# A fused attention and expert kernel: where four kinds of products stand in each place of the turn, and one half of the router's transposes a turn later

## The reference, cut to what matters

```python
h = jnp.concatenate([_L0_tok_ref(x, ...), txt], axis=1)          # 8 x 384 x 256
n = _layernorm(h)
c_kv = n @ W_DKV ; k = c_kv @ W_UK ; v = c_kv @ W_UV ; q = n @ W_UQ
probs = softmax(where(causal, q @ k.T / sqrt(16), -inf))         # 16 heads of 16
h = h + (probs @ v) @ W_O
m = _layernorm(h)
scores = softmax(m @ router_w) ; the two best of 8 experts for each token
h = h + sum over the two of weight * expert(m) + bias            # 384 slots an expert and choice
```

## Time and profile before

| | before |
|---|---|
| median of 3 runs | 693.08 us (690.37 to 693.27) |
| the profiled execution's own time | 693.07 us |
| its span | 691.3 us |
| TensorE busy | 622.6 us, 90% of the span |
| VectorE / ScalarE / GpSimd busy | 407.3 / 374.7 / 386.3 us |
| chain that ended last, TensorE's share | 64% |

### The profile page before, as it was taken

How to read it: one execution, slowest core, us unless ns; L and a number is a source line. 1 busy time by engine, 2 the same in 40 slices (tenths; PEclk the granted TensorE clock), 3 DMA queues, 4 the chain that set the end, 5 groups by cost and what they waited for, 6 DMA issues and landing times.

```text
span 691.3 us, 13802 instructions
## 1 busy us (share of the span) xinstructions
PE 622.6 (90%) x5104; PEld 510.8 (74%) x5104; DVE 407.3 (59%) x1005; ACT 374.7 (54%) x800; POOL 386.3 (56%) x605
## 2 busy tenths in 40 slices
PE   2888999998989999998878699999999999999990
PEld 2554565565656666565657699999999999999990
DVE  4787686797987979669737144444444444444310
ACT  4456776757676575665541355555544455554430
POOL 3403233336463454546474588888888888887222
PEclk9999999999999999999989899999999999999996
DMA  7339274533423232343121532444444444442222
GB/s 263 100 104 259 67 197 151 171 101 114 136 81 94 74 94 82 96 145 129 35 69 67 185 126 32 101 110 108 105 107 108 107 107 107 106 105 46 23 26 27
DMA packets 66476, 73.73 MB, mean 107 GB/s; under 512 B 6312, under 2 KB 61458, under 8 KB 66408
## 3 DMA queue, kind: packets, MB, share of 16 engines
q1 hardware_dynamic: 55584, 59.27, 28.4%
q0 software_dynamic: 9504, 13.00, 11.1%
q10 hardware_dynamic: 1320, 0.57, 0.3%
HBM read 31.62 MB, written 22.35 MB: 78 GB/s over the span
## 4 chain that ended last, share of the span: by engine, by line
PE 64%; DVE 6%; ACT 5%; issue 5%; POOL 3%; DMA 2%; SPq 1%; ACTq 0%; DVEq 0%; POOLq 0%
PE t_bank L1643 19%; PE bank L1658 12%; PE s_bank L1658 6%; PE bank L669 5%; PE t_bank L634 3%; PE s_bank L612 3%; PE t_bank L727 2%; PE t_bank L697 2%; PE s_bank L1629 2%; DVE mx L1100 1%; SPq L400 1%; PE s_bank L613 1%; PE bank L681 1%; ACT part L975 1%; PE bank L759 1%
## 5 line engine op out<-in xcount | busy, mean ns | idle before, releaser
L1602 DVE TENSOR_TENSOR hl<-h,hh 128x384 fp32r<-128x384 f32 x128 | 102.8, 804 | 157.4 <-ACT h L1560 157.4
L537 POOL TENSOR_SCALAR_AFFINE_SELECT pt<-pt 128x256 f32<-128x256 f32 x192 | 80.3, 423 | 162.6 <-ACT pt L916 126.5
L1100 DVE TENSOR_REDUCE mx<-s_bank 128x2 f32<-128x256 f32 (+2 forms) x192 | 121.9, 681 | 39.3 <-PE s_bank L613 39.0
L1557 ACT ACTIVATE hh<-t_bank 128x384 fp32r<-128x384 f32 x128 | 63.0, 492 | 133.7 <-PE t_bank L1643 131.5
L1527 POOL DMA_INDIRECT out<-yo,xr x48 | 76.0, 1583 | 70.2 <-ACT yo L1568 57.8
L916 ACT ACTIVATE pt<-t_bank 128x512 f32<-128x512 f32 x128 | 76.1, 602 | 56.1 <-PE t_bank L634 54.1
L1515 POOL TENSOR_TENSOR wl<-wr,wh 128x256 fp32r<-128x256 f32 x112 | 94.5, 879 | 1.2
L1643 PE MATMUL t_bank<-xh,wh 128*128 128x384 f32 x256 | 87.2, 340 | 0.0
L1643 PE MATMUL t_bank<-xl,wh 128*128 128x384 f32 x256 | 86.7, 338 | 0.0
L1643 PE MATMUL t_bank<-xh,wl 128*128 128x384 f32 x256 | 86.6, 338 | 0.0
L612 PE MATMUL s_bank<-ks,qs 96*128 96x128 bf16 (+2 forms) x384 | 78.7, 274 | 5.0 <-DVE mx L1100 4.2
(11 more groups left out here) (188 smaller groups left out, 1363.4 us busy)
## 6 DMA issues: line engine op xcount, KB each, us to landing
wr<-in_w SPq DMA_DIRECT2D x16, 1024.0 KB, 5.9
qs<-part SPq DMA_DIRECT2D x96, 96.0 KB
ks<-part SPq DMA_DIRECT2D x90, 96.0 KB
slot_rows<-empty SPq DMA_DIRECT2D x4, 1560.0 KB, 9.1
xr<-slot_rows SPq DMA_DIRECT2D x16, 390.0 KB, 3.3
wr<-in_x SPq DMA_DIRECT2D x8, 768.0 KB, 5.8
out<-hid SPq DMA_DIRECT2D x8, 384.0 KB
qs<-mT ACTq DMA_DIRECT2D x64, 3.0 KB
```

Source lines behind the costliest of these rows:

```text
L537: pool.affine_select(out=blocks, in_=blocks, compare_op=ALU.is_ge, fill=0.0, base=0, pattern=[[0, 2], [1, P]], channel_multiplier=-1).then ...
L1100: ins = dve.tensor_reduce(mx[:, p // 2, j, 2 * (p % 2):2 * (p % 2) + 2], pair_region(s_bank, j), AX_X, ALU.max)
L1602: dve.tensor_tensor(hl[:, f, :], h[f % 2][:, :], hh[:, f, :].bitcast(F32), ALU.subtract).then_inc(hl_done, 1)
```

## The change

Three edits, made alike in TensorE's and ScalarE's loops:

1. In the tensor program the calls of `latents(b + 2, 1)` and `query_key(*ahead(n, p, 0))` move from behind `maxima`, `ranks`, `router` and `contexts_back` to ahead of them, right behind the first third of the shifted scores.
2. In the scalar program the copies of these products stand right behind the exponentials of the first third, ahead of the copy of the maxima.
3. `rows_back(b, 1)`, the second half of the transposes for the router, moves from place 3 of an odd turn to place 0 of the next even turn, on both engines, for all items but the last.

No instruction is added or taken away.

```diff
@@ tensor
                 if cur:
                     shifted_scores(n, p, 0)
 
+                if odd and p == 1 and late(b + 2):
+                    latents(b + 2, 1)
+                if ahead(n, p, 0):
+                    query_key(*ahead(n, p, 0))
                 if p == 0 and cur:
                     maxima(n, 1)
                 if p == 1:
...
                     if cur:
                         contexts_back(n, 0, False)
-                if odd and p == 1 and late(b + 2):
-                    latents(b + 2, 1)
-                if ahead(n, p, 0):
-                    query_key(*ahead(n, p, 0))
...
                 if ahead(n, p, 1):
                     query_key(*ahead(n, p, 1))
+                if not odd and p == 0 and live(b - 2) and b - 2 < B - 1:
+                    rows_back(b - 2, 1)
...
-                    if p == 3 and live(b - 1):
+                    if p == 3 and b - 1 == B - 1:
                         rows_back(b - 1, 1)
@@ scalar
                 if cur:
                     exps(n, p, 0)
 
+                if odd and p == 1 and late(b + 2):
+                    latents(b + 2, 1)
+                if ahead(n, p, 0):
+                    query_key(*ahead(n, p, 0))
                 if p == 0 and cur:
                     maxima(n, 1)
                 if p == 2 and nxt:
                     maxima(n + 1, 0)
-                if odd and p == 1 and late(b + 2):
-                    latents(b + 2, 1)
-                if ahead(n, p, 0):
-                    query_key(*ahead(n, p, 0))
...
+                if not odd and p == 0 and live(b - 2) and b - 2 < B - 1:
+                    rows_back(b - 2, 1)
...
-                if odd and p == 3 and live(b - 1):
+                if odd and p == 3 and b - 1 == B - 1:
                     rows_back(b - 1, 1)
```

## The result

| kernel | median, us | range, us | runs | ratio to before, 95% |
|---|---|---|---|---|
| before | 691.91 | 690.37 to 693.54 | 13 | |
| changed | 689.92 | 687.63 to 694.77 | 13 | 0.9967 [0.9951, 0.9982] |

The change makes the kernel faster, by 0.33%, some 2 us. The time lies inside the range and above the 687.5 that was forecast: the direction was right, the gain was forecast at 5.5 us and is less than half of that. By the prediction's own limit of 0.5% this counts as the same time, to which it had given 0.28.

The account below looks back on a forecast made before the run. TensorE was taken as the bound, busy 38.58 of 41.62 us an item, with 12.0 us of reachable waits. Gains of 3.4 + 1.0 + 1.5 - 0.36 = 5.5 us took 693.07 to 687.5; range for 8 in 10 runs 684.0 to 691.6.

Parts of the forecast that it names:

- item 2: Turns 1 and 2, no `rows_back` yet: shorter waits at L732 and L727 gain 0.24 + 0.37 + 0.37 = 1.0 us.
- items 3 to 6: Four steady-state items ahead, each gaining 0.24 + 0.60 = 0.84 us, 3.4 us together.
- item 7 and turn 14: Item 7, turns 11 and 12, gains 1.5 us; turns 13 to 14 lose 0.36 to transposes with no gain.
- the forecast's own signs: Values expected in the profile after: period of two turns, and TensorE's waits at L747, L732, L612 (0.9) and L712.
- The two turns of about 40.8: Steady state: two turns, one item, were to take about 40.8 us instead of 41.62.
- Order, places 1 and 2 and the exchange at place 0: Odd turn: 0.37 gained at place 2, 0.13 lost at place 1, net 0.24; `part` ahead of `mT` at place 0, 0.37.
- the paragraph on the even turn: Claimed the 0.84 us gained ahead of VectorE's even-turn run is kept, since that run starts when TensorE's scores come.
- Moving `rows_back`: From place 3 of the odd to place 0 of the even turn: 0.60 an item less 0.37 for the exchange, 0.23.
- the paragraph on the rule: Turn change: `ms` taken as in time, though VectorE and GpSimd shutting each other out could lengthen it to 1.15 us.
- the first rival: Change of turns: VectorE's run with `ms` holds TensorE, moving `rows_back` gives nothing; gain 2.2 us, 690.9 us; chance 0.20.
- The even turn: absorbed: Place 2 gain of 0.37 us only lengthens the scores' wait for VectorE at place 3, 0.55 to about 0.9; counted nothing.
- The clock: Rival: one slow TensorE stretch more or fewer moves time 1.4 us either way, 686.1 or 688.9; no separate chance, widens each.

Follow-up runs that it names:

- full change, bias on VectorE: Changed kernel with GpSimd's three bias additions an item, items 0 to 6, made one VectorE operation at place 0 of the even turn; 688.42 us, 0.9894 of before.
- edits 1 and 2 alone: Changed kernel with the move of `rows_back` undone, so only the products and their copies come earlier; 688.35 us, 0.9939 of before.
- edit 3 alone: Kernel before with only the second half of `rows_back` moved one turn later, order of products unchanged; 690.5 us, 0.997 of before.
- GpSimd's additions were thin: Changed kernel with GpSimd's bias additions cut from 256 columns to 16 for items 0 to 6, for diagnosis only; 687.18 us, 0.9887 of before.
- the curve later: Changed kernel with the bias additions on VectorE, and VectorE's curve moved from place 1 to place 2, behind the maxima; 692.53 us, 0.9964 of before.
- Filling the wait: Changed kernel with 26 unused TensorE products ahead of the scores of place 3 in even turns 2 to 10; 690.03 us, 0.9967 of before.
- the second profile of the same kernel: Profile from measuring the unaltered changed kernel again, beside the follow-up kernels on their chip; 693.13 us, 0.9971 of before.
- the second set: Runs on one chip of before (695.07 us), the changed kernel again, and it with additions thin, bias on VectorE, or latents back behind `ranks` and `contexts_back` (691.51 us).
- the kernel with the later additions: Changed kernel with GpSimd's bias additions moved from place 3 of the odd turn to place 2 of the next even turn; 696.69 us, 1.0066 of before.

## Why the prediction was right in direction and too large

The gains on TensorE by stretches, from the starts of its latents and of the products of turn 14, in us:

| stretch | forecast | full change | full change, bias on VectorE |
|---|---|---|---|
| item 2 | 1.0 | 1.03 | 1.02 |
| items 3 to 6 | 3.4 | 0.53 | 2.78 |
| item 7 and turn 14 | 1.5 - 0.36 = 1.1 | 0.47 | 2.07 |
| sum | 5.5 | 2.03 | 5.87 |

The full change's 0.53 holds a slow stretch of 1.34 (42.83 against 41.49), which the third column does not have. So without the conflict and without a slow stretch the sum comes out near the forecast, but by two errors that cancel: the steady items give less than was forecast and the last one more.

**The waits that it aimed at.** By the forecast's own signs: L747 for `rowT` from 3.2 to near 0.3, measured 0.5; L732 for `part` from 6.9 to about 4, measured 3.6; the new wait of L712 for `xnT` 0.3 six times, measured 1.7 in 6. All three stand. The two turns of about 40.8 do not: 41.01 in the steady state where the subtraction is not hit, and 41.5 where it is.

**Order, places 1 and 2 and the exchange at place 0: 0.24 + 0.37 = 0.61 forecast, 0.34 measured** (41.62 to 41.28). The terms of TensorE's own order stand. Set before beside edits 1 and 2 alone, instruction by instruction: the same work starts 3.10 earlier ahead of the latents (190.57 and 187.47), 2.94 behind them (195.11 and 192.17), 3.27 after the exchange at place 2 (198.02 and 194.75) and 3.62 after the one at place 0 (207.51 and 203.89). That is -0.16, +0.33 and +0.35, where -0.13, +0.37 and +0.37 were forecast. When VectorE begins its run of the even turn (215.05 and 211.37) 0.58 is there. Behind its curve (220.69 and 217.24) 0.35 is left. So what failed is the sentence in the paragraph on the even turn that the gain "is kept, because VectorE starts that run when TensorE's scores come": VectorE starts earlier, but its run takes 0.23 longer. From the second steady item on the curve takes 2.15 (the line at 213.52 above) in each kernel that has edits 1 and 2 and neither the curve nor the additions moved beside it, and 1.61 in before and with edit 3 alone; L1179 behind it gives 0.31 back. In before GpSimd's masks begin when the curve is done, in the full change they lie over its second instruction. VectorE's curve in before, GpSimd's masks in before and in the full change:

```profile
218.08 1.61 DVE L1155 SCALAR_TENSOR_TENSOR wr<-r,curve_w,wr 128x512 f32<-128x512 f32 x2
```

```profile
219.71 0.77 POOL L537 TENSOR_SCALAR_AFFINE_SELECT pt<-pt 128x256 f32<-128x256 f32 x2
```

```profile
214.34 0.77 POOL L537 TENSOR_SCALAR_AFFINE_SELECT pt<-pt 128x256 f32<-128x256 f32 x2
```

No run moved the masks, so that they are the reason is not shown.

**Moving `rows_back`: 0.23 forecast, 0.26 measured,** alone. This term stands.

**Item 2, the first: 1.0 forecast, 1.0 measured** (from 38.84 to 37.81 between its latents and the next). **Item 7 and turn 14: 1.1 forecast, 0.5 measured,** from the latents at 274.65 and 271.38 to the products of turn 14 at 326.69 and 322.95. The 1.92 of `ms` at 283.49 lies in it. With the bias on VectorE it is 2.1: the subtraction was long here in before too (0.81 at 286.87, 1.15 at 324.56), and the prediction took that as given.

**The step that failed most** is in the paragraph on the rule: "By the rows of the steady turns `ms` is in time and my sum stands." In the profiles it cost 2.5 us (the last paragraph of this section). I took the subtraction's 0.15 to 0.3 of before for granted at its new time. The rule weighed there, of the Trainium skill, page "SBUF — State Buffer", section "Who interferes with whom", was the one that held: 0.15 became 1.41, 1.44 and 1.92, and 0.15 again in the steady turns of the kernels where GpSimd's additions were thin or gone (0.38 at most with the curve later too). Where the subtraction is hit, a period is 41.49, longer than the 41.28 of edits 1 and 2 alone: edit 3 gives nothing there, as the first rival says, and a little less than nothing. Its time, 690.9, is nearest to the measured one, and the range held because it had been drawn around that rival as well. The rival's reason was VectorE's load; what holds TensorE is one subtraction made long by GpSimd. I had also gone through the two edits one by one and had not asked what stood in front of L642 after both.

**The even turn: absorbed, and more than that.** Forecast was a wait at place 3 of 0.9 instead of 0.55; it is 1.65 (217.69), in all 10.0 us instead of 4.2. VectorE works almost without a gap from 210.49 to 217.6. In edits 1 and 2 alone the wait is 1.65 too, 1.10 more than in before. Of these 0.87 are what TensorE gains between the start of VectorE's run and place 3, sized at 0.37 in the forecast and rightly counted as nothing; 0.23 are VectorE's longer run and a true loss.

**The clock.** I gave it 1.4 us either way and said that the change opens no stretch of idling in the steady turns. It does: behind the 1.65 at 217.69 the products of 218.38 to 221 are slow in this profile (the eight of L697 take 2.54, 1.97 elsewhere), some 1.3 us. Filling the wait doesn't change the median. The slow stretch is in another turn in the second profile of the same kernel: the eight products are slow at 220.71 in the first, and in the second at 181.56, one item earlier, while those of the same turn (223.73) are not. The Trainium skill, page "TensorE: Matmul & The Clock Gate", section "What's actually happening", says that the same kernel gets a different number of slow matmuls from run to run. Both profiles agree that it varies: the turn differs between them.

**What stays open.** By the ratios the conflict costs 0.6% to 0.7%, 4 to 5 us. What the profiles show of it is 0.47 in each of two steady periods (41.49 and 41.02), and 1.6 in item 7 with turn 14, where the subtraction is hit in any order (1.15 at 320.30): 2.5 us. A part of the rest is the clock: over all runs of the second set the mean granted clock was 0.976 for the full change, 0.980 with the additions thin and 0.979 with the bias on VectorE. Among the runs at 0.977 or 0.978 the full change took 693.3 us on average (3 runs) and the two others 689.4 (4 runs), so 3.9 us of the difference are there at the same clock. Where the 1.4 us between that and the 2.5 lie, no run shows. Nor is it settled what holds the subtraction from 200.40 to 200.70, where only a mask (200.33) runs on GpSimd, and a mask alone did not make it long in the kernel with thin additions.

## What to carry to other kernels

Two edits that each gain by themselves can share one cover: before taking work from in front of a matmul, list what it hides of every other operand of that matmul, at the times that the other edits will give. A tiny operation of VectorE with two inputs in the chain that feeds TensorE is worth more protection than its 0.15 us suggest; look where GpSimd's long instructions lie in the new order, and if they can't be moved off it, put them on VectorE itself (0.9971 became 0.9894 with one operation more on the busier engine). When a change is worth less than its parts, run the parts: edits 1 and 2 alone were worth nearly twice the whole.

## What the runs showed of the hardware that was not expected

- A subtraction of 12 columns (0.15 us) next to GpSimd additions of 0.73 us took 1.41 to 1.92 us. The longest lies over two of them (283.49 to 285.41, additions from 283.61 and 284.66): the subtraction does not get in between one addition and the next.
- Three waits of TensorE of 3.5 us, and one of 1.87, in the kernel with the later additions were each followed by a stretch of slow products (the eight of L697 took 2.48 to 2.93, 1.97 at full clock). Waits of 1.65 were followed by one in some turns and not in others. The granted clock falls where the products are slow: it was 0.57 from 218.0 to 221.5 in the changed kernel's profile, and one such stretch cost 1.34 us.
- VectorE's curve, two instructions with two inputs, takes 1.61 us or 2.15 by where it falls against GpSimd's masks (2.15 where two of them, 0.77 us, lie over its second instruction), and 3.54 where two of the additions lie over it. The first of these was seen and not tested.
